# ScalarE takes Q's high part ahead of two casts in the steps of an attention head loop

## The chip, the cores and the metric

The kernel runs on one core of a Trainium2 chip. The metric is the device time of one execution in microseconds (us); for several executions the median stands.

## What is computed

Four layers run one after the other, each with a layer norm ahead of it and a residual behind it, on x of 2 x 512 x 256: an attention with 3 heads of width 256, a feed-forward layer with ternary weights, a causal attention with 16 heads of width 128, and a product in int8. The change lies in the third:

```
q = einsum('bpd,hde->bphe', x, W_Q) + b_Q        # k and v alike
scores = einsum('bqhe,bkhe->bhqk', q, k) / sqrt(128)
scores = where(causal, scores, -100000.0)
attn = softmax(scores, axis=-1)
z = einsum('bkhe,bhqk->bqhe', v, attn)
out = einsum('bqhe,hed->bqd', z, W_O) + b_O
```

## The kernel before

Every product of fp32 numbers is made of three passes over numbers that are split into a high and a low part (`split_mm`, L401 to L403): high with high, low with high, high with low. ScalarE writes the high part (a rounded copy), VectorE or GpSimd subtracts it from the source to get the low part. TensorE needs both.

The third layer runs in 32 steps, `window(w)`, w = 0 to 31: one head of one batch half in each. Inside a step no order is left to a scheduler: for TensorE, ScalarE and VectorE a list of marks (`PE_ORDER`, `ACT_ORDER`, `DVE_ORDER`) says what each does, one after the other; each engine has one queue and waits on semaphores in it. Steps 1 to 25 are the steady ones. The marks that count here, for step w:

- S0 to S3: the scores of step w+1, four blocks of 128 rows with 128 to 512 columns. TensorE multiplies (L689 to L696), VectorE masks them and takes the maximum (`max1`, L1483, tile SM), ScalarE takes the exponential (`exp1`, L963, tile PR).
- Q0, K1, V2: the projections for step w+2. TensorE multiplies (`project_qk`, `project_v`), ScalarE writes the high part (`project_hi`, Q_hi and K_parts on L957, V_hi on L954), VectorE the low part (`project_lo`, L1468, V_lo on L1465, which comes one step later as W2). Two PSUM banks take turns, so a projection waits until the low part of the one before the last is written: V2 waits for Q_lo of its own step, K1 for V_lo of the step before.
- C3, C2, C1, C0: the high parts of the turned probabilities of step w-1 (`moved_hi`, L974, PT_hi from MV). C3 waits for the transfer that brings MV. GpSimd writes the low parts in the same order (`moved_low`, L1154, PT_lo).
- B0: the attention product of step w-1 (`attend`), which waits for all four low parts; then ScalarE writes Z_hi (L980) and VectorE Z_lo (Z0 of the next step).
- U0 to U3: VectorE turns blocks of normalised probabilities into BT (`turn_blocks`, L1502). SP stores BT to DRAM and loads it back turned, as MV, one step later (L446, L452). GpSimd normalises ahead of that (`normalise`, L1138 to L1147).
- O0: the output projection of an earlier step. G0 to G3: in some steps VectorE splits weights of the next pair of heads (`load_a`, L1404 to L1408, `load_b`), GpSimd writes a part of their low halves (`split_a`, L1110) behind PT_lo and ahead of the normalisation. K's and V's projections wait for those.

TensorE's order in a steady step is S0 Q0 S1 S2 O0 K1 S3 V2 B0 (no O0 in steps 1 and 2), ScalarE's is S0 C3 C2 Q0 S1 C1 C0 S2 K1 S3 V2 B0, VectorE's begins S0 Z0 U2 U3 W2 S1 Q0 S2. A step starts here with S0 on TensorE. Step 7 starts at 249.47 us, step 8 at 258.72, step 9 at 268.61.

Of the kernel before, what the change touches and what calls it, by code (L numbers as in the profile page):

```python
# [63 lines left out]
def build(nc, x, wq0, wk0, wv0, fcT, fcb, wupT, wgateT, wdownT, pack1, bias_all, bo1, qw, qb, out):  # L64
    ctx = ExitStack()
    with ctx:
# [190 lines left out]
        def steps(text):  # L257
            return [(step[0], int(step[1])) for step in text.split()]
# [1 line left out]
        FIRST_MOVED, LAST_MOVED = 0, WINDOWS - 7  # L260
        STEADY_PE = (steps("S0 Q0 S1 S2 O0 K1 S3 V2 B0"),
                     steps("S0 Q0 S1 S2 O0 K1 S3 V2 B0"))
        STEADY_ACT = (steps("S0 C3 C2 Q0 S1 C1 C0 S2 K1 S3 V2 B0"),
                      steps("S0 C3 C2 Q0 S1 C1 C0 S2 K1 S3 V2 B0"))
        STEADY_DVE = (steps("S0 Z0 U2 U3 W2 S1 Q0 S2 O0 G0 G1 G2 G3 R0 S3 K1 U0 U1 R1"),
                      steps("S0 Z0 U2 U3 W2 S1 Q0 S2 O0 G0 G1 G3 R0 S3 K1 G2 U0 U1 R1"))
        EVEN_PE = steps("T0 T1 S0 O0 T2 T3 S1 Q0 S2 O1 K1 A0 S3 V2")
# [11 lines left out]
            WINDOWS - 2: steps("T0 T1 S0 S1 O0 S2 T2 T3 S3 O1"),  # L279
            WINDOWS - 1: steps("T0 T1 B0 T2 A0 T3 O0 A1 O1 I0 I1")}  # L280
        ACT_ORDER = {w: STEADY_ACT[w % 2] for w in range(1, LAST_MOVED + 1)} | {
            1: steps("S0 C3 C2 Q0 S1 C1 C0 S2 K1 S3 V2 B0"),
            0: steps("W2 S0 S1 Q0 S2 K1 S3 V2"),
            WINDOWS - 6: steps("T0 T1 S0 C3 C2 C1 C0 S1 T2 Q0 S2 T3 K1 B0 S3 A0"),
            WINDOWS - 5: EVEN_ACT,
# [1436 lines left out]
```

## Time and profile before

| | us |
|---|---|
| three runs: median (lowest, highest) | 506.07 (506.07, 508.27) |
| the profiled execution | 507.92 |
| its span, first to last instruction | 506.1 |
| TensorE, VectorE, ScalarE, GpSimd busy | 482.0, 379.1, 293.5, 281.9 |

The granted clock of TensorE is 0.994 of full speed on average. In a row of the order in time the columns are start, duration, engine, line and operation, output and input tiles, partitions x elements, count; in brackets stands the idle time before it and what ended it. In a row of waits: who waited for whom, us in total, how often, the longest.

### The profile page before, as it was taken

The numbers are of one execution on the slowest core, as the hardware profiler recorded it, in microseconds if no ns is written. First come the engines' busy times: TensorE is split into PE (matmuls) and PEld (weight loads), VectorE is DVE, ScalarE is ACT, GpSimd is POOL, SyncE is SP. The second block draws the span as 40 slices with busy tenths as digits, with TensorE's granted clock in tenths as the row PEclk, the third lists the DMA queues.
The fourth block names the chain that finished last, engine by engine and source line by source line (L and its number), as shares of the span: only waits on it lengthen the run. The fifth ranks groups of instructions, "written<-read, shape, count | busy, mean of one in ns | idle before, by whom it ended". The sixth has DMA issues, their size and how long they took to land.

```text
span 506.1 us, 8910 instructions
## 1 busy us (share of the span) xinstructions
PE 482.0 (95%) x3020; PEld 429.4 (85%) x3020; DVE 379.1 (75%) x967; ACT 293.5 (58%) x690; POOL 281.9 (56%) x378
## 2 busy tenths in 40 slices
PE   8999999999999978899999999999999989999973
PEld 7888998899888856789989989999889989899962
DVE  2676886775746577778878878888778896677887
ACT  2356336535454646586667667776766756655643
POOL 1344234422755456686677677786677796512243
PEclk9999999999999999999999999999999999999997
DMA  8900000000010017565665665655765645000002
GB/s 270 378 29 2 1 0 1 0 1 1 24 41 1 0 53 185 157 179 143 180 178 148 182 171 148 192 169 139 205 163 154 192 140 156 2 1 1 2 0 83
DMA packets 54380, 51.58 MB, mean 102 GB/s; under 512 B 3520, under 2 KB 49728, under 8 KB 54336
## 3 DMA queue, kind: packets, MB, share of 16 engines
q1 hardware_dynamic: 53248, 49.98, 34.4%
q10 hardware_dynamic: 1088, 1.05, 0.6%
q8 instruction: 24, 0.39, 0.3%
q14 instruction: 20, 0.16, 0.1%
HBM read 32.92 MB, written 18.09 MB: 101 GB/s over the span
## 4 chain that ended last, share of the span: by engine, by line
PE 68%; DVE 11%; DMA 7%; POOL 4%; issue 4%; ACT 4%; SPq 1%; DVEq 0%; POOLq 0%; ACTq 0%
PE bank L401 18%; PE bank L403 17%; PE bank L402 17%; DMA MV<-turned_dram 3%; PE bank L696 2%; PE bank L694 2%; PE bank L695 2%; POOL HID_lo L1123 2%; DMA turned_dram<-BT 2%; DMA Wv_sb<-wv 2%; DVE SM L1483 1%; PE bank L624 1%; PE bank L623 1%; ACT E L882 1%; DVE XN L1212 1%
## 5 line engine op out<-in xcount | busy, mean ns | idle before, releaser
L1154 POOL TENSOR_TENSOR PT_lo<-MV,PT_hi 128x512 fp32r<-128x512 f32 (+1 forms) x104 | 91.3, 910 | 51.9 <-ACT PT_hi L974 51.7
L963 ACT ACTIVATE PR<-SM,nmax 128x128 f32<-128x128 f32 (+3 forms) x128 | 72.0, 563 | 64.2 <-DVE nmax L1483 63.4
L1099 POOL TENSOR_TENSOR E_lo<-E,E_hi 128x512 fp32r<-128x512 f32 x24 | 31.0, 1295 | 53.7 <-ACT E_hi L887 46.6
L1483 DVE CUSTOM_DVE_ANT_0 SM<-bank,causal 128x384 f32<-128x384 f32 (+3 forms) x102 | 53.9, 529 | 8.8 <-PE bank L696 6.7
L401 PE MATMUL bank<-XT_hi,W_hi 128*128 128x512 f32 x128 | 52.3, 408 | 5.5 <-DVE V_lo L1465 4.1
L974 ACT CAST PT_hi<-MV 128x512 fp32r<-128x512 f32 (+1 forms) x104 | 42.1, 453 | 20.0 <-DMA MV<-turned_dram 19.8
L1502 DVE STREAM_TRANSPOSE BT<-PR 128x128 f32<-128x128 f32 (+1 forms) x104 | 48.1, 492 | 6.3 <-POOL PR L1138 4.6
L403 PE MATMUL bank<-XT_hi,W_lo 128*128 128x512 f32 x128 | 50.5, 394 | 0.0
L402 PE MATMUL bank<-XT_lo,W_hi 128*128 128x512 f32 x128 | 50.2, 392 | 0.0
L403 PE MATMUL bank<-PT_hi,V_lo 128*128 128x128 f32 (+3 forms) x130 | 41.5, 319 | 0.0
L402 PE MATMUL bank<-PT_lo,V_hi 128*128 128x128 f32 (+3 forms) x130 | 41.5, 319 | 0.0
L401 PE MATMUL bank<-PT_hi,V_hi 128*128 128x128 f32 (+3 forms) x130 | 40.5, 312 | 0.9 <-POOL PT_lo L1154 0.7
L882 ACT ACTIVATE E<-bank,nmax 128x512 f32<-128x512 f32 x24 | 16.5, 687 | 41.5 <-DVE nmax L1285 41.3
L401 PE MATMUL bank<-W_hi,XT_hi 128*128 128x256 f32 x128 | 36.3, 283 | 2.3 <-DVE Q_lo L1468 2.1
L401 PE MATMUL bank<-WO_hi,Z_hi 128*128 128x256 f32 x128 | 36.0, 282 | 2.0 <-DVE Z_lo L1517 2.0
L1468 DVE SCALAR_TENSOR_TENSOR Q_lo<-bank,bias,Q_hi 128x512 fp32r<-128x512 f32 x32 | 24.0, 749 | 17.3 <-ACT Q_hi L957 17.0
L402 PE MATMUL bank<-W_lo,XT_hi 128*128 128x256 f32 x128 | 35.7, 279 | 0.0
L403 PE MATMUL bank<-W_hi,XT_lo 128*128 128x256 f32 x128 | 35.7, 279 | 0.0
L403 PE MATMUL bank<-WO_hi,Z_lo 128*128 128x256 f32 x128 | 35.6, 278 | 0.0
L402 PE MATMUL bank<-WO_lo,Z_hi 128*128 128x256 f32 x128 | 35.6, 278 | 0.0
L694 PE MATMUL bank<-K_parts,Q_hi 128*128 128x384 f32 (+3 forms) x102 | 34.9, 342 | 0.0
L980 ACT ACTIVATE Z_hi<-bank,bias 128x512 fp32r<-128x512 f32 x31 | 21.4, 689 | 21.9 <-PE bank L403 21.9
(186 smaller groups left out, 1599.2 us busy)
## 6 DMA issues: line engine op xcount, KB each, us to landing
MV<-turned_dram SPq DMA_DIRECT2D x104, 160.0 KB, 3.2
turned_dram<-BT SPq DMA_DIRECT2D x26, 384.0 KB, 3.0
stage<-pack SPq DMA_DIRECT2D x32, 256.0 KB, 3.9
turned_dram<-BT SPq DMA_DIRECT2D x26, 256.0 KB, 3.3
X<-x SPq DMA_DIRECT2D x2, 512.0 KB, 8.9
wraw<-wupT SPq DMA_DIRECT2D x1, 1024.0 KB, 9.2
wraw<-wgateT SPq DMA_DIRECT2D x1, 1024.0 KB, 11.1
wraw<-wdownT SPq DMA_DIRECT2D x1, 1024.0 KB, 13.4
```

The lines of the kernel that those rows point to most:

```text
L401: pe.matmul(dst, a_hi, b_hi, start=first, stop=False, skip_group_check=share)
L402: pe.matmul(dst, a_hi, b_lo, start=False, stop=False, skip_group_check=share)
L403: return pe.matmul(dst, a_lo, b_hi, start=False, stop=last, skip_group_check=share)
L694: pe.matmul(dst[:, 0:n], Q_hi[:, slot, cols], K_hi[:, slot, 0:n], start=True, stop=False)
L882: act.activation(E0[:, m, :], bank[i % 3][:], ACT.Exp, bias=nmax0[:, m:m + 1], scale=1.0, accum_out=sum0[:, m:m + 1]).then_inc(s0_exp, 1)
L963: act.activation(PR[:, c, 0:(c + 1) * P], SM[:, c % 2, 0:(c + 1) * P], ACT.Exp, bias=nmax1[:, c:c + 1], scale=-1.0, accum_out=sum1[:, c:c ...
L974: act.copy(by_quad(PT_hi[w % 2], c), moved_part(w, c)).then_inc(mv_hi, 1)
L1099: pool.tensor_tensor(E0_lo[:, m, :], E0[:, m, :], E0_hi[:, m, :], ALU.subtract).then_inc(e0_lo, 1)
L1154: pool.tensor_tensor(by_quad(PT_lo[w % 2], c), moved_part(w, c), by_quad(PT_hi[w % 2], c), ALU.subtract).then_inc(mv_lo, 1)
L1468: ins = dve.scalar_tensor_tensor(lo[:, w % 2, :], src, bias1[:, p, 2 * which + h:2 * which + h + 1], hi[:, w % 2, :], ALU.add, ALU.subtract)
L1483: dve.tensor_tensor_reduce(SM[:, c % 2, 0:n], s_bank(w, c)[:, 0:n], mask, 1.0, HIGHEST, ALU.add, ALU.min, nmax1[:, c:c + 1]).then_inc(s_ma ...
L1502: dve.transpose(BT[w % 2][:, :, moved_blocks(c), :].rearrange("p j b c -> p b j c"), PR[:, c, 0:(c + 1) * P].rearrange("p (b j c) -> p b j ...
```

## The change

In the lists of ScalarE for steps 1 to 25, Q0 moves from behind C3 and C2 to the place ahead of them. The other engines' lists stay, and so do all instructions and semaphores. Step 0 and steps 26 to 31 have lists of their own, which stay.

```diff
-        STEADY_ACT = (steps("S0 C3 C2 Q0 S1 C1 C0 S2 K1 S3 V2 B0"),
-                      steps("S0 C3 C2 Q0 S1 C1 C0 S2 K1 S3 V2 B0"))
+        STEADY_ACT = (steps("S0 Q0 C3 C2 S1 C1 C0 S2 K1 S3 V2 B0"),
+                      steps("S0 Q0 C3 C2 S1 C1 C0 S2 K1 S3 V2 B0"))
...
         ACT_ORDER = {w: STEADY_ACT[w % 2] for w in range(1, LAST_MOVED + 1)} | {
-            1: steps("S0 C3 C2 Q0 S1 C1 C0 S2 K1 S3 V2 B0"),
+            1: steps("S0 Q0 C3 C2 S1 C1 C0 S2 K1 S3 V2 B0"),
```

## Rows read from the trace of the kernel before

**Rows 1.** Busy time by engine, from the page: us, share, instructions.

```profile
PE 482.0 (95%) x3020; PEld 429.4 (85%) x3020; DVE 379.1 (75%) x967; ACT 293.5 (58%) x690; POOL 281.9 (56%) x378
```

**Rows 2.** Waits of TensorE over the span.

```profile
PE bank L401 <- DVE V_lo L1465: 4.2, 5, 1.5
PE bank L401 <- DVE Q_lo L1468: 2.1, 4, 1.1
...
PE bank L401 <- POOL PT_lo L1154: 0.7, 2, 0.6
```

**Rows 3.** Waits of all engines over the span.

```profile
ACT PT_hi L974 <- DMA MV<-turned_dram: 19.8, 20, 2.2
...
DVE Q_lo L1468 <- ACT Q_hi L957: 17.0, 15, 2.4
```

**Rows 4.** Steps 8 and 7 as stretches: bounds, length, busy time of each engine.

```profile
258.72:268.61 9.89, 9.69 (x62) 8.47 (x61) 7.64 (x22) 6.36 (x16) 6.52 (x11) 1.00 0.84 221
249.47:258.72 9.25, 9.25 (x62) 8.47 (x61) 7.22 (x19) 6.37 (x16) 5.71 (x9) 1.00 0.60 170
```

**Rows 5.** Order in time: end of step 7 (first row), then step 8.

```profile
256.87 0.39 PE L401 MATMUL bank<-PT_hi,V_hi 128*128 128x512 f32 x1
...
262.51 1.03 ACT L974 CAST PT_hi<-MV 128x512 fp32r<-128x512 f32 x2 [2.15 <-DMA MV<-turned_dram]
...
263.21 3.38 POOL L1154 TENSOR_TENSOR PT_lo<-MV,PT_hi 128x512 fp32r<-128x512 f32 x4 [2.93 <-ACT PT_hi L974]
...
263.45 0.68 ACT L957 ACTIVATE Q_hi<-bank,bias 128x512 fp32r<-128x512 f32 x1
...
264.17 0.75 DVE L1468 SCALAR_TENSOR_TENSOR Q_lo<-bank,bias,Q_hi 128x512 fp32r<-128x512 f32 x1 [1.68 <-ACT Q_hi L957]
...
265.07 0.36 PE L401 MATMUL bank<-W_hi,XT_hi 128*128 128x256 f32 x1 [0.20 <-DVE Q_lo L1468]
...
266.64 0.51 PE L401 MATMUL bank<-PT_hi,V_hi 128*128 128x512 f32 x1
```

**Rows 6.** Order in time: step 9; the first row is the last matmul of Q0.

```profile
270.04 0.39 PE L403 MATMUL bank<-XT_hi,W_lo 128*128 128x512 f32 x1
...
270.15 1.02 ACT L974 CAST PT_hi<-MV 128x512 fp32r<-128x512 f32 x2
...
272.42 0.51 ACT L963 ACTIVATE PR<-SM,nmax 128x256 f32<-128x256 f32 x1 [0.66 <-DVE nmax L1483]
...
270.84 2.27 POOL L1154 TENSOR_TENSOR PT_lo<-MV,PT_hi 128x512 fp32r<-128x512 f32 x2 [1.52 <-ACT PT_hi L974]
273.39 1.38 POOL L1154 TENSOR_TENSOR PT_lo<-MV,PT_hi 128x256 fp32r<-128x256 f32 x2 [0.28 <-ACT PT_hi L974]
275.73 1.31 POOL L1110 TENSOR_TENSOR W_lo<-stage,W_hi 128x512 fp32r<-128x512 f32 x1 [0.97 <-DVE W_hi L1408]
...
276.04 0.39 PE L401 MATMUL bank<-PT_hi,V_hi 128*128 128x512 f32 x1
```

**Rows 7.** Order in time: step 5, its first two casts and GpSimd's weight split.

```profile
232.68 1.03 ACT L974 CAST PT_hi<-MV 128x512 fp32r<-128x512 f32 x2
...
238.11 1.31 POOL L1110 TENSOR_TENSOR W_lo<-stage,W_hi 128x512 fp32r<-128x512 f32 x1 [0.97 <-DVE W_hi L1408]
```

**Rows 8.** Order in time: steps 1 and 2; last, one piece of the chain.

```profile
196.05 4.01 POOL L1154 TENSOR_TENSOR PT_lo<-MV,PT_hi 128x512 fp32r<-128x512 f32 x4 [2.53 <-ACT PT_hi L974]
...
197.00 0.75 DVE L1468 SCALAR_TENSOR_TENSOR Q_lo<-bank,bias,Q_hi 128x512 fp32r<-128x512 f32 x1 [1.82 <-ACT Q_hi L957]
...
200.42 1.30 POOL L1110 TENSOR_TENSOR W_lo<-stage,W_hi 128x512 fp32r<-128x512 f32 x1 [0.36 <-DVE W_hi L1408]
...
206.24 0.47 PE L401 MATMUL bank<-XT_hi,W_hi 128*128 128x512 f32 x1 [1.46 <-DVE V_lo L1465]
...
210.12 5.31 DMA MV<-turned_dram
```

**Rows 9.** Order in time: step 24 on TensorE.

```profile
414.42 0.47 PE L401 MATMUL bank<-XT_hi,W_hi 128*128 128x512 f32 x1 [1.29 <-DVE V_lo L1465]
```

## Prediction

> **What bounds the kernel now.** I read the page's busy shares first, then the waits of TensorE, then the waits of all engines, then the busy time of single steps, and last the order in time on each engine inside four steps. TensorE is busy 95% of the span [rows 1], so a moved ScalarE instruction can only buy back idle time of TensorE. The waits of TensorE are short: 4.2 us for V's low part (5 times), 2.1 us for Q's low part (4 times), 0.7 us for the low part of the probabilities (2 times) [rows 2]. The other engines look much worse: VectorE waits 17.0 us for ScalarE's Q_hi, in 15 steps, and ScalarE's casts wait 19.8 us for the moved probabilities, in 20 of 26 steps [rows 3]. The first of these is what the change is aimed at: Q_hi stands in ScalarE's queue behind casts that wait for a transfer, although Q's product has long been there.
>
> A step that waits for nothing takes 9.25 us (step 7), step 8 took 9.89 us [rows 4]. TensorE reaches the attention product, the last of its step, 256.87 - 249.47 = 7.40 us after the start in step 7 [rows 4, 5]. Step 8 starts at 258.72. Its casts start at 262.51, 3.79 us in, after 2.15 us of waiting for the transfer; Q_hi follows at 263.45, Q_lo at 264.17 after 1.68 us of idle VectorE, and V's projection at 265.07, held 0.20 us by Q_lo [rows 5]. So far this reads like a stall that the change removes. But GpSimd works on PT_lo from 263.21 for 3.38 us, to 266.59, and the attention product starts at 266.64 [rows 5]. Of the two things that the attention product needs, PT_lo is the later. The casts lead to it with a fixed lag: 266.64 - 262.51 = 4.13 us. The limit follows: a cast that starts more than 7.40 - 4.13 = 3.27 us after its step's start delays TensorE, and a V projection 0.2 us earlier only waits longer at the next instruction.
>
> **What the change removes, adds and moves.** Nothing is added or removed. In steps 1 to 25 Q_hi goes ahead of two casts. The casts are busy 1.03 us, yet Q_hi starts 263.45 - 262.51 = 0.94 us after them, so neighbours overlap by 0.09 us, and Q_hi with its 0.68 us pushes what follows by 0.59 us [rows 5]. ScalarE issues no transfer there, so no queue of SP or GpSimd is passed. New is a wait: both casts now stand behind Q's projection on TensorE.
>
> *Steps with a late transfer* (1, 3, 8, 12, 18, 20: the casts wait longest there, 2.2 us at most [rows 3]). Q's projection ends about 1.83 us into a step (in step 9 its last matmul ends at 270.04 + 0.39 = 270.43, start 268.61 [rows 4, 6]). Q_hi then falls into the 2.15 us that ScalarE idled, and the casts start with the landing as before. V's projection no longer waits, PT_lo ends at the same time. Gain: 0. VectorE is freed up to 1.7 us earlier, which nobody on the path needs, with one exception below. It stays at zero while the casts lead to the attention product with the 4.13 us.
>
> *Steps with an early transfer.* Step 9 is the extreme: the casts ran without a wait at 270.15, 1.54 us in. Now Q_hi comes first. For the hand-over from TensorE I take the 0.05 us that lie between PT_lo's end and the attention product in step 8 [rows 5]; the casts start at 270.43 + 0.05 + 0.59 = 271.07, 2.46 us in, 0.92 us later. That is 0.8 us under the limit of 3.27, so TensorE does not see it. What else is late? The exponentials of S1 start at 272.42 because they wait for VectorE, while the casts end at 272.1: not moved. GpSimd starts 0.92 us later, 270.84 + 0.92 = 271.76, its first two instructions end 2.27 us later at 274.03; the 0.28 us wait before the last two is swallowed, and it ends at 274.03 + 1.38 = 275.41. In this step GpSimd next splits a weight at 275.73, and it had waited 0.97 us for VectorE's W_hi before that [rows 6]. So even there 0.3 us of cover is left, and the attention product (276.04) has 0.6 us. Step 5 starts at 249.47 - 2 x 9.25 = 230.97; its casts move from 232.68 to 233.43, by 0.75 us, and GpSimd had waited 0.97 us as well [rows 7]: 0.2 us of cover, the smallest; 13, 17, 21 and 23 have more. Cost: 0, and if the cover were gone, the price is in the slower rival.
>
> *The exception, step 1.* Q_lo waits 1.82 us for Q_hi (197.00), and behind it on VectorE stand the weight splits of this step. GpSimd ends PT_lo at 196.05 + 4.01 = 200.06, but starts its weight split at 200.42, because W_hi comes late; from there it goes to the turned blocks, V_lo of step 2, and TensorE stands still 1.46 us before 206.24 [rows 8]. With Q_lo 1.8 us earlier W_hi is there in time, and the split starts with the end of PT_lo: 0.36 - 0.02 = 0.34 us earlier. The same chain leads on into the store and the transfer that step 3 waits for (5.31 us in the chain [rows 8]), so the 0.34 us are kept through step 3. The bounds are 0, if PT_lo ends later by as much, and 1.46 us, the whole stall. I take 0.34, since PT_lo's end at 200.06 stands directly behind.
>
> *Step 24.* A like stall of 1.29 us stands here before K's projection [rows 9]. Its transfer was early, and in step 23, where the chain begins, I find no wait of Q_lo. Bounds 0 and 0.1 us; I take 0.
>
> Sum: 0.34 us, in round figures 0.4 with the few hundredths of step 24. The profiled execution took 507.92 us (span 506.1, 1.8 us around it) and would take 507.5. It is 1.85 us above the median of the three runs, 506.07; the same subtraction gives 505.7.
>
> The port between VectorE and GpSimd is the one size that I can't read off. In step 1 PT_lo took 4.01 us and in step 8, with no weight split on VectorE, 3.38 us [rows 5, 8]: a difference of 0.63 us. The Trainium skill (SBUF — State Buffer, Who interferes with whom) says that "A DVE instruction with two SBUF inputs contends with a GpSimd instruction that reads SBUF"; the two durations agree with it, and as the splits move 1.8 us earlier, by that rule they still fall inside PT_lo and only meet other instructions of it.
>
> **The rivals.**
>
> *Q_lo is what bounds (0.08).* For it: the page names Q_lo as the releaser of TensorE. Of the 2.1 us the longest (1.1 us) lies in step 0, whose order is not changed [rows 2]. 1.0 us are left, and with the 0.4: 504.7 us. Against it speaks PT_lo's end in step 8.
>
> *Transfers fall otherwise (0.11).* A landing decides six steps. In the chain it took 5.31 us at step 3 [rows 8]. If the shifted start lets them land early, each gives back 0.5 us (7.92 against 7.40 in step 8), 3 us in all: 503.1 us (0.07). If as many land later by the same, 508.7 us (0.04). No row speaks for either, the stores hang on TensorE's own pace.
>
> *The port (0.10).* Splits and PT_lo of step 1 cost each other 0.63 us more or less: 505.1 to 506.3 us. Moving the splits does not take them out of PT_lo's time, so the middle is kept.
>
> *Nothing is moved that matters (0.05).* 506.1 us.
>
> *Slower: the casts come too late (0.06).* Place: behind Q_hi in the steps with early transfers. Point of decision: casts more than 3.27 us into the step delay the attention product; in the weight steps 5, 9, 13, 17, 21 already 0.2 to 0.3 us beyond my time make GpSimd late for the turned blocks, and then V_lo late for K's projection. With the hand-over 1 us longer than taken, GpSimd is 0.7 us late. I estimate that half of it reaches TensorE in five steps and all of it in step 24, where V_lo is already late: 5 x 0.35 + 0.7 = 2.5 us, plus 0.2 us in some of the others: 508.9 us with the gain of step 1 gone. For it: the smallest cover is a few tenths. Against it: Q_hi's start is fixed by TensorE, which is steady.
>
> **How the numbers follow.** The forecast itself has 0.60, at 505.7 us, with 505.3 to 506.1 from its own bounds. The three runs of before lie 2.2 us apart, which belongs into the range as well. It reaches down past 504.7, not to 503.1, and up past the port's 506.3, not to 508.7: 504.2 to 507.6 us. A difference under 0.5% (2.5 us) cannot be told from no change for this kernel. Only the early landings are faster by more, 0.07; slower by more are the slower rival and the late landings, 0.09; within is 0.84.
>
> **What would show it.** Right: Q_hi starts about 1.9 us into every step from 1 to 25; the wait of VectorE for Q_hi falls from 17.0 us to 5 or 6, what lies before and behind the changed steps; TensorE's wait for Q_lo falls to the 1.1 us of step 0, and a wait for PT_lo (4.13 us behind the casts) stands in its place in steps 8, 12, 18 and 20; the casts never start before 2.4 us in; GpSimd's split in step 1 starts directly behind PT_lo, and the stall in step 2 is 1.1 us. Wrong: PT_lo ends after 7.3 us in a step whose transfer was early; the stall in step 24 over 1.3 us; the casts of step 8 starting elsewhere than 3.8 us in.

## The result

The change makes the kernel slower by 0.22%: the median of 20 runs is 507.48 us against 507.01 us for 20 runs of the kernel before, the ratio 1.0022 (95% interval 1.0012 to 1.0033). By that ratio the loss is about 1.1 us, in place of the 0.3 to 0.4 us gained that were forecast; it is not the ratio of the two medians, which lie only 0.47 us apart (the means lie 0.93 us apart). The profiled execution of the changed kernel took 506.95 us with a span of 505.2 us, 1.0 us less than the profiled one of before. Single executions of either kernel lie 2.5 to 3 us apart, so the time of one says nothing here; what can be read in one are the steps.

TensorE is as busy as before, and its waits have changed places. These are the lines that answer to [rows 1] to [rows 3]; the columns are the same.

```profile
PE 481.3 (95%) x3020; PEld 430.0 (85%) x3020; DVE 384.2 (76%) x967; ACT 293.9 (58%) x690; POOL 281.8 (56%) x378
```

```profile
PE bank L401 <- DVE V_lo L1465: 4.3, 7, 1.4
...
PE bank L401 <- POOL PT_lo L1154: 1.2, 2, 0.7
PE bank L401 <- DVE Q_lo L1468: 1.1, 1, 1.1
```

```profile
DVE Q_lo L1468 <- ACT Q_hi L957: 5.5, 5, 2.4
...
ACT PT_hi L974 <- DMA MV<-turned_dram: 4.8, 7, 1.4
```

The waits that the change aims at are nearly gone. TensorE waits for Q_lo once, in step 0 (2.1 us and 4 times before), and VectorE waits 5.5 us for Q_hi in place of 17.0. But TensorE waits 7 times for V_lo in place of 5, and VectorE is busy 384.2 us in place of 379.1, although it has the same 967 instructions. That is where to look: two of its lines take 4.8 of the 5.1 us. For L1404, the first split of weights, the view of one line gives the lowest, the median and the longest duration in ns; first the kernel before, then the changed one.

```profile
L1404 DVE TENSOR_SCALAR W_hi<-stage x8: 409/420/562, 133.5 to 405.4; 128x512 fp32r<-128x512 f32 x8
```

```profile
L1404 DVE TENSOR_SCALAR W_hi<-stage x8: 414/970/989, 133.4 to 404.2; 128x512 fp32r<-128x512 f32 x8
```

The same instruction takes 0.96 to 0.99 us in steps 5, 9, 13, 17, 21 and 23, in place of 0.42 (0.53 and 0.56 in steps 21 and 23). The other line is the cast of W_O's weights, L1417: 0.99, 0.87, 0.99 and 0.97 us in steps 3, 7, 15 and 19, where it took 0.51 to 0.57. Again before, then changed:

```profile
L1417 DVE CAST WO_hi<-stage x8: 412/530/575, 187.0 to 433.1; 128x512 fp32r<-128x512 f32 x8
```

```profile
L1417 DVE CAST WO_hi<-stage x8: 414/710/987, 186.9 to 432.3; 128x512 fp32r<-128x512 f32 x8
```

This one costs TensorE nothing that shows: steps 4 and 8, behind two of the slow casts, took 9.25 and 9.29 us; steps 16 and 20 were longer, with late transfers. The loss comes with L1404. Step 9 of the changed kernel, in order of time by engine (it starts at 266.42; [rows 6] answer to it):

```profile
268.28 0.69 ACT L957 ACTIVATE Q_hi<-bank,bias 128x512 fp32r<-128x512 f32 x1 [0.23 <-PE bank L403]
268.87 1.02 ACT L974 CAST PT_hi<-MV 128x512 fp32r<-128x512 f32 x2
270.23 0.51 ACT L963 ACTIVATE PR<-SM,nmax 128x256 f32<-128x256 f32 x1 [0.34 <-DVE nmax L1483]
...
269.56 3.57 POOL L1154 TENSOR_TENSOR PT_lo<-MV,PT_hi 128x512 fp32r<-128x512 f32 x4 [3.08 <-ACT PT_hi L974]
...
271.79 1.34 POOL L1154 TENSOR_TENSOR PT_lo<-MV,PT_hi 128x256 fp32r<-128x256 f32 x2
...
274.10 1.30 POOL L1110 TENSOR_TENSOR W_lo<-stage,W_hi 128x512 fp32r<-128x512 f32 x1 [0.97 <-DVE W_hi L1408]
...
271.85 0.96 DVE L1404 TENSOR_SCALAR W_hi<-stage 128x512 fp32r<-128x512 f32 x1
272.85 0.83 DVE L1406 SCALAR_TENSOR_TENSOR W_lo<-stage,W_hi 128x512 fp32r<-128x512 f32 x1
273.60 0.41 DVE L1408 CAST W_hi<-stage 128x512 fp32r<-128x512 f32 x1
...
279.11 0.65 DVE L1465 TENSOR_TENSOR V_lo<-bank,V_hi 128x512 fp32r<-128x512 f32 x1
```

The casts start 2.45 us in, GpSimd's third piece of PT_lo at 271.79, and VectorE's weight split at 271.85, 0.06 us behind it; the split takes 0.54 us more. Before, VectorE reached the same place, 5.42 us into the step, with GpSimd's third piece nearly through (it began at 273.39, 4.78 us in [rows 6]). GpSimd does not even see its own lateness: it still waits 0.97 us for W_hi, as before, only that W_hi comes 0.54 us later. From there everything is late: GpSimd's normalisation, the turned blocks, and V_lo of step 10, which ends at 279.76. K's projection starts there at 279.91, 4.21 us in; in the kernel before it starts 3.97 us into that step. First the changed kernel, then the one before:

```profile
279.91 0.47 PE L401 MATMUL bank<-XT_hi,W_hi 128*128 128x512 f32 x1
```

```profile
281.86 0.40 PE L401 MATMUL bank<-XT_hi,W_hi 128*128 128x512 f32 x1
```

The stretches show it too: steps 8 and 10 of the changed kernel, then step 10 of the kernel before.

```profile
257.13:266.42 9.29, 9.29 (x62) 8.50 (x61) 7.53 (x22) 6.60 (x16) 7.23 (x13) 1.00 0.68 193
...
275.70:285.29 9.59, 9.52 (x62) 8.56 (x61) 7.82 (x23) 6.55 (x17) 9.11 (x15) 1.00 0.57 162
```

```profile
277.89:287.18 9.29, 9.29 (x62) 8.50 (x61) 7.56 (x23) 6.48 (x16) 8.56 (x14) 1.00 0.66 175
```

Steps 6, 10, 14, 18 and 22, each behind a step with weight splits, took 9.68, 9.59, 9.62, 9.63 and 9.64 us from start to start, where a step that waits for nothing takes 9.25 to 9.29: 1.8 us in all. In steps 14 and 18 the casts were late as well (3.52 and 3.55 us in), so a part of their loss would be there without the collision. The stall of step 24 went from 1.29 [rows 9] to 1.37 us.

```profile
413.63 0.47 PE L401 MATMUL bank<-XT_hi,W_hi 128*128 128x512 f32 x1 [1.37 <-DVE V_lo L1465]
```

Step 1, the one with the forecast gain, answers to [rows 8]:

```profile
195.01 4.19 POOL L1154 TENSOR_TENSOR PT_lo<-MV,PT_hi 128x512 fp32r<-128x512 f32 x4 [1.61 <-ACT PT_hi L974]
199.17 1.29 POOL L1110 TENSOR_TENSOR W_lo<-stage,W_hi 128x512 fp32r<-128x512 f32 x1
...
204.96 0.47 PE L401 MATMUL bank<-XT_hi,W_hi 128*128 128x512 f32 x1 [1.03 <-DVE V_lo L1465]
```

GpSimd's split follows PT_lo at once, and the stall of step 2 shrank from 1.46 to 1.03 us. But PT_lo takes 0.18 us longer there, 4.19 us in place of 4.01.

### The profile page after: what moved, and what is told of

It reads as the page before. It is cut to its first block, busy times and chain, and to the rows that moved or that the text cites. A ratio compares the mean times of both kernels' runs of the same rounds, so it can differ in the third digit from the quotient of the medians.

```text
span 505.2 us, 8910 instructions
## 1 busy us (share of the span) xinstructions
PE 481.3 (95%) x3020; PEld 430.0 (85%) x3020; DVE 384.2 (76%) x967; ACT 293.9 (58%) x690; POOL 281.8 (56%) x378
## 4 chain that ended last, share of the span: by engine, by line
PE 61%; DVE 16%; POOL 7%; DMA 5%; issue 5%; ACT 4%; SPq 1%; DVEq 0%; POOLq 0%; ACTq 0%
PE bank L401 17%; PE bank L402 16%; PE bank L403 16%; POOL HID_lo L1123 2%; POOL PT_lo L1154 2%; PE bank L696 2%; PE bank L694 2%; PE bank L695 2%; DMA turned_dram<-BT 2%; DVE SM L1483 2%; DVE BT L1502 2%; DMA Wv_sb<-wv 2%; DMA MV<-turned_dram 2%; DVE V_lo L1465 1%; ACT PR L963 1%
## 5 line engine op out<-in xcount | busy, mean ns | idle before, releaser
L694 PE MATMUL bank<-K_parts,Q_hi 128*128 128x384 f32 (+3 forms) x102 | 34.9, 342 | 0.0
L695 PE MATMUL bank<-K_parts,Q_hi 128*128 128x384 f32 (+3 forms) x102 | 34.0, 334 | 0.0
```

Of the source, the lines that this page charges most:

```text
L694: pe.matmul(dst[:, 0:n], Q_hi[:, slot, cols], K_hi[:, slot, 0:n], start=True, stop=False)
L695: pe.matmul(dst[:, 0:n], Q_hi[:, slot, cols], K_lo[:, slot, 0:n], start=False, stop=False)
```

## The experiments

Theory A (port): GpSimd's third piece of PT_lo, later because the casts are later, blocks VectorE's first weight split; VectorE's lateness makes V_lo late one step on. Against it: B, the new order costs a little in every step; C, transfers land later; D, it is Q_hi and Q_lo being early that hurts; and the plainest one, GpSimd's own lateness, without VectorE. All ratios are to the kernel before, which ran in turn with them on the same chip. In the edited kernels the line numbers of the same instructions are a few higher.

### One part of the change: all steps but the weight steps

```diff
+        ACT_ORDER |= {w: steps("S0 C3 C2 Q0 S1 C1 C0 S2 K1 S3 V2 B0") for w in (5, 9, 13, 17, 21, 23)}
```

> Q0 goes ahead of C3 and C2 in all steps of 1 to 25 but 5, 9, 13, 17, 21 and 23, in which VectorE splits weights. Theory A (port): in the changed kernel GpSimd is still busy with the third piece of PT_lo when VectorE starts the first weight split (L1404), which then takes 0.97 us in place of 0.42; V_lo of the next step is late by as much, and TensorE loses 0.3 to 0.4 us in steps 6, 10, 14, 18 and 22, 1.9 us in all with step 24. Here L1404 stays at 0.42 us in these steps, steps 6, 10, 14, 18 and 22 take 9.25 to 9.3 us unless a transfer is late, and the time is that of the changed kernel less 1.9 us: 0.5 to 1 us under the kernel before, ratio about 0.998. Rival B (order): the casts behind Q0 cost a little in every step; then this has some 19/25 of the loss of the changed kernel, ratio about 1.0015. Rival C (transfers): the loss is in landings that fall later; ratio about 1.002, with more steps in which the attention product waits for PT_lo.

Measured: ratio 0.9985 (0.9965 to 1.0004), 506.73 us. The median of that line is 418 ns. Steps 6, 10, 18 and 22 took 9.29, 9.28, 9.28 and 9.31 us, step 14 took 9.78 with a late transfer. The loss is gone with six of 25 steps; that speaks against B and C, whose 1.0015 and 1.002 lie outside the interval. L1417 still takes 0.97 to 0.99 us in steps 3, 11, 15 and 19 of this kernel, so it is not what cost the time.

### The other part: the weight steps alone

```diff
+        ACT_ORDER |= {w: steps("S0 Q0 C3 C2 S1 C1 C0 S2 K1 S3 V2 B0") for w in (5, 9, 13, 17, 21, 23)}
```

> The counterpart: Q0 goes ahead of the casts in steps 5, 9, 13, 17, 21 and 23 alone. Theory A (port): L1404 takes 0.97 us in these six, the steps behind them are 0.3 to 0.4 us longer, and the time is 1.9 us over the kernel before, ratio about 1.0035 to 1.004, more than the changed kernel has. Rival B (order): 6/25 of the loss of the changed kernel, ratio about 1.0005. Rival C (transfers): no more than 1.001.

Measured: ratio 1.0016 (0.9995 to 1.0037), 508.32 us against 506.93. The steps show theory A, all five with early transfers:

```profile
L1405 DVE TENSOR_SCALAR W_hi<-stage x8: 410/966/990, 133.9 to 405.6; 128x512 fp32r<-128x512 f32 x8
```

```profile
239.89:249.50 9.61, 9.54 (x61) 8.59 (x61) 7.82 (x23) 6.57 (x17) 9.12 (x15) 1.00 0.54 149
277.50:287.15 9.65, 9.46 (x61) 8.51 (x61) 7.87 (x24) 6.74 (x17) 9.14 (x15) 1.00 0.59 162
315.01:324.60 9.59, 9.52 (x62) 8.56 (x61) 7.82 (x23) 6.68 (x17) 9.11 (x15) 1.00 0.61 163
352.79:362.38 9.59, 9.51 (x61) 8.55 (x61) 7.83 (x23) 6.57 (x17) 9.11 (x15) 1.00 0.57 158
390.50:400.16 9.66, 9.46 (x62) 8.51 (x61) 7.88 (x24) 6.63 (x17) 9.18 (x15) 1.00 0.59 160
```

These are steps 6, 10, 14, 18 and 22: 1.7 us above 9.28 together. The ratio is below the forecast of 1.0035, with that inside its interval; by itself it settles nothing.

### The casts late, Q_hi late as well

```diff
+        ACT_ORDER |= {w: steps("S0 E0 C3 C2 Q0 S1 C1 C0 S2 K1 S3 V2 B0") for w in (5, 9, 13, 17, 21, 23)}
...
+                    elif kind == "E":
+                        act.wait_ge(pj_psum, 3 * (w + 2) + 1)
+                        act.activation(XN[:, 0:2, :].rearrange("p t d -> p (t d)"), causal[:], ACT.Identity,
+                                       bias=bias1[:, 0, 0:1], scale=1.0)
```

> The order of the kernel before, but in steps 5, 9, 13, 17, 21 and 23 ScalarE does one more instruction ahead of C3 and C2: it waits for Q0's product as Q_hi does and has its shape (128x512, Identity with a bias), but reads a constant and writes a tile that nobody reads. Q_hi stays behind the casts. So the casts are as late as in the changed kernel, about 2.47 us into the step, and Q_hi is not early. Theory A (port): what counts is that the casts, and with them PT_lo, are later: L1404 takes 0.97 us as in the changed kernel, steps 6, 10, 14, 18, 22 are longer by 0.3 to 0.4 us (or more, as Q_lo is late too), ratio 1.0035 or more. Rival D: the loss comes from Q_hi and Q_lo being early (VectorE then does other work beside GpSimd): L1404 stays at 0.42 us and the ratio at 1.000.

Measured: ratio 1.0028 (1.0008 to 1.0047), and steps 6, 10, 14, 18 and 22 took 9.77, 9.68, 9.62, 9.81 and 9.72 us. But L1404 (here L1409) took 0.55 us, not 0.97: a miss. Step 5 of this kernel starts at 229.26:

```profile
233.39 0.75 DVE L1473 SCALAR_TENSOR_TENSOR Q_lo<-bank,bias,Q_hi 128x512 fp32r<-128x512 f32 x1 [0.36 <-ACT Q_hi L958]
...
235.13 0.55 DVE L1409 TENSOR_SCALAR W_hi<-stage 128x512 fp32r<-128x512 f32 x1
```

Q_lo waited, VectorE came to the split 5.87 us in, 0.44 us later than in the other kernels, and GpSimd's piece was nearly through. 0.44 us of start and 0.13 us of duration make 0.57 us, as much as the collision costs. So this run does not tell A from a plain lateness of VectorE. It shows the second half of the chain: some 0.55 us lost on VectorE by the end of the first split, from whatever cause, costs TensorE 0.34 to 0.44 us one step on (steps 10, 14 and 22; in steps 6 and 18 the casts came 3.65 and 3.71 us in as well). Nor does it decide on rival D: Q_lo is late here, which is a cause of its own.

### Less work for GpSimd in the changed kernel

This kernel leaves out most of the last two pieces of PT_lo in the weight steps; it keeps low parts of an earlier step there.

```diff
-                    pool.tensor_tensor(by_quad(PT_lo[w % 2], c), moved_part(w, c), by_quad(PT_hi[w % 2], c),
-                                       ALU.subtract).then_inc(mv_lo, 1)
+                    n = 1 if c < 2 and w + 1 in (5, 9, 13, 17, 21, 23) else QUAD
+                    pool.tensor_tensor(by_quad(PT_lo[w % 2], c)[:, :, :, 0:n], moved_part(w, c)[:, :, :, 0:n],
+                                       by_quad(PT_hi[w % 2], c)[:, :, :, 0:n], ALU.subtract).then_inc(mv_lo, 1)
```

> The changed kernel, in which GpSimd leaves out most of the two last pieces of PT_lo (blocks of 256 and 128 columns: one column of 32 is kept in each) in steps 5, 9, 13, 17, 21 and 23, so that these low parts are those of an earlier step. The casts are as late as in the changed kernel, but GpSimd is done with PT_lo about 1 us earlier. Theory A (port): VectorE's first weight split starts at 5.43 us into the step and finds GpSimd idle, takes 0.42 to 0.5 us, and the stalls of steps 6, 10, 14, 18 and 22 go: 1.9 us less than the changed kernel, ratio to the kernel before about 0.998. Rival B or D (the order on ScalarE itself, or Q being early): the late V_lo stays, ratio about 1.002.

Measured: ratio 0.9976 (0.9959 to 0.9994), 505.77 us. Step 9 starts at 267.89; the split is 5.43 us in, as in the changed kernel, and takes 0.45 us:

```profile
271.04 2.79 POOL L1155 TENSOR_TENSOR PT_lo<-MV,PT_hi 128x512 fp32r<-128x512 f32 x4 [3.08 <-ACT PT_hi L974]
```

```profile
273.32 0.45 DVE L1405 TENSOR_SCALAR W_hi<-stage 128x512 fp32r<-128x512 f32 x1
```

Steps 6, 10, 14, 18 and 22 took 9.24 to 9.29 us. ScalarE's order and the times of its casts are those of the changed kernel, and Q_hi is as early as there (Q_lo starts 3.69 us into step 9 in this kernel, in the changed one and in the one before), so what cost the time is GpSimd's work beside the split. Rivals B and D fall here.

### More work for GpSimd in the kernel before

```diff
+                    if c == 2 and w + 1 in (5, 9, 13, 17, 21, 23):
+                        pool.tensor_tensor(XN[:, 2, 0:240].rearrange("p (b i q) -> p b i q", b=3, i=CT), moved_part(w, c)[:, :, :, 0:20],
+                                           by_quad(PT_hi[w % 2], c)[:, :, :, 0:20], ALU.subtract)
```

> The kernel before, with ScalarE's order untouched: only GpSimd does one subtraction more between the first and the second piece of PT_lo in steps 5, 9, 13, 17, 21 and 23 (240 columns, into a tile that nobody reads, some 0.7 us). So GpSimd's third piece begins ahead of VectorE's first weight split (5.43 us into the step), as in the changed kernel, but the casts and Q_hi keep their times. GpSimd itself has 0.97 us of waiting ahead of its own weight split, so its lateness alone is covered. Theory A (port): L1404 takes 0.85 to 1.0 us in place of 0.42, steps 6, 10, 14, 18 and 22 take 9.6 us in place of 9.25, ratio to the kernel before 1.003 to 1.004. Rival D or B (the loss comes with ScalarE's order): L1404 stays at 0.42, the steps at 9.25 and the ratio at 1.000.

Measured: L1404 took 0.94, 1.00, 0.73, 0.72 and 1.02 us in steps 5, 9, 13, 17 and 21, and steps 6, 10, 14, 18 and 22 took 9.60, 9.66, 9.40, 9.39 and 9.64 us: the longer the split, the longer the step behind it. In step 23 the split took 0.52 us (0.56 before), but the two behind it 1.11 and 0.68. Step 9, with GpSimd's third piece of PT_lo in the last row:

```profile
271.20 0.70 POOL L1155 TENSOR_TENSOR XN<-MV,PT_hi 128x240 f32<-128x240 f32 x1
271.86 2.32 POOL L1157 TENSOR_TENSOR PT_lo<-MV,PT_hi 128x384 fp32r<-128x384 f32 x3
...
272.83 0.75 POOL L1157 TENSOR_TENSOR PT_lo<-MV,PT_hi 128x256 fp32r<-128x256 f32 x1
```

```profile
272.86 1.00 DVE L1407 TENSOR_SCALAR W_hi<-stage 128x512 fp32r<-128x512 f32 x1
```

ScalarE's order is the old one and Q_lo has its old times, and the collision and its price are back. GpSimd's own lateness is covered: PT_lo ends 6.75 us into step 9, and GpSimd still waits until 7.71 for VectorE's W_hi. That settles the last rival. The ratio is 1.0014 (0.9996 to 1.0032), where the five steps, 1.3 us over 9.28, would make 1.0026; that lies inside. Its expectation of 0.85 to 1.0 us was missed in steps 13 and 17, where the casts were earliest and VectorE came later into GpSimd's piece.

Six traces (the kernel before, the changed one twice, and the second, third and fifth experiment) give this as a series. When the split started 0.00 to 0.07 us behind the start of GpSimd's third piece it took 0.96 to 1.02 us; 0.09 behind, 0.94; 0.30 to 0.32 behind, 0.72 or 0.73; 0.46 to 0.49 behind, 0.53 to 0.57; 0.64 or 0.65 behind, 0.42. Each time it ended 1.01 to 1.07 us behind the start of that piece, which itself is recorded with 0.73 to 0.76 us. The end of the split is set by the piece and not by its own start, as of an instruction that stands still until the piece is done.

### Cover for the chain: the second split on ScalarE

ScalarE idles 1.5 us behind K_hi in step 9, and 2.05 us in the changed kernel. Two kernels let it do the cast of L1408 for K's weights there, one with the new order, one with the old.

```diff
+        for w in (1, 5, 9, 13, 17, 21, 23):
+            at = ACT_ORDER[w].index(("K", 1)) + 1
+            ACT_ORDER[w] = ACT_ORDER[w][:at] + [("G", 1)] + ACT_ORDER[w][at:]
...
+                        act.wait_ge(ld_pack[1], 16 * q + 16)
+                        act.copy(W_hi[q % 2][:, 1, :, :].rearrange("p k e -> p (k e)"),
+                                 stage[:, W_COLS:2 * W_COLS]).then_inc(wa_act, 1)
```

VectorE leaves this cast out, and GpSimd waits for ScalarE's signal (`wa_act`) in its place.

> The changed kernel, and the high part of K's weights in steps 1, 5, 9, 13, 17, 21 and 23 is cast by ScalarE behind K_hi (it idles 2 us there) and not by VectorE (L1408, second of the three splits). L1404 is still hit by GpSimd. Theory A: it still takes 0.97 us, but VectorE has 0.4 us less to do behind it and GpSimd's weight split starts 0.8 us earlier, so that V_lo of the next step is in time: steps 6, 10, 14, 18 and 22 take 9.25 to 9.3 us, the stall of step 24 shrinks from 1.4 to about 0.8 us, that of step 2 by 0.3. Ratio to the kernel before 0.995 to 0.998. Rival B (the order costs by itself, away from the weight splits): those steps stay at 9.6 us, ratio 1.001 or more.

> The same move of the cast to ScalarE, with ScalarE's old order (C3, C2 ahead of Q0). Theory A: steps 6, 10, 14, 18 and 22 had no stall and gain nothing; the stalls of steps 24 and 2 shrink by 0.3 to 0.6 us each: ratio to the kernel before 0.998. If with this cover the new order is at least as fast as the old one, then it was the cover, not the order, that the change lost on: e6 is then 0.5 to 1 us under e7, what the order gives in step 1 and in the steps with late transfers.

Measured: new order 0.9978 (0.9957 to 0.9999), old order 0.9959 (0.9938 to 0.9981). With the new order the split still takes 0.97 us, steps 10, 14 and 22 took 9.28 or 9.29 us, and step 24 stalls 0.35 us for V_lo, but a new wait of 0.65 us for K_lo stands at its start. Steps 6 and 18 took 10.14 and 9.45; in step 6 TensorE waited 0.62 us for PT_lo behind a late transfer, and in step 18 the casts came 3.35 us in, past the 3.27 of the prediction, and the attention product 4.15 us behind them. Where the wait for K_lo comes from was not found out. With the old order GpSimd's weight split starts earlier, as it was meant to:

```profile
274.90 1.30 POOL L1122 TENSOR_TENSOR W_lo<-stage,W_hi 128x512 fp32r<-128x512 f32 x1 [0.67 <-ACT W_hi L1045]
```

So the lost time can be covered, but with the cover the new order was not found faster than the old one, where 0.5 to 1 us had been expected; the two intervals overlap.

### Does the new order give anything where it does no harm?

The first edit (all steps but the weight steps) with the cover, beside the old order with the cover and the changed kernel, on one chip.

> Two edits together: Q0 ahead of the casts in all steps of 1 to 25 but 5, 9, 13, 17, 21 and 23 (as in the first experiment), and the high part of K's weights cast by ScalarE behind K_hi in steps 1, 5, 9, 13, 17, 21 and 23. No collision at L1404 (0.42 to 0.56 us), no stall in steps 6 to 22, the stall of step 24 at 0.8 us. If the new order is worth anything by itself where it does no harm, this is 0.3 to 1 us faster than the same with the old order, ratio to the kernel before 0.994 to 0.996; if it is worth nothing there (the casts lead to the attention product, whatever Q does), it equals it, ratio 0.996.

> The old order with K's weights cast on ScalarE once more, beside the others on one chip: ratio to the kernel before 0.996, as before, 0.994 to 0.998.

> The changed kernel once more, on the same chip as the two before it: ratio 1.002, L1404 at 0.97 us in steps 5, 9, 13, 17, 21 and 23, steps 6, 10, 14, 18 and 22 at 9.6 us in this execution too, since the collision comes from fixed times inside a step and not from transfers.

Measured: 0.9977 (0.9958 to 0.9995) with the new order in the calm steps, 0.9964 (0.9944 to 0.9984) with the old one, 1.0022 (1.0001 to 1.0043) for the changed kernel; medians 505.72, 505.13 and 508.22 us. The new order gives nothing that can be measured in the steps other than these six. In this execution of the changed kernel the median of L1404 is 965 ns again, and steps 6, 10, 14, 18 and 22 took 9.54, 9.61, 9.60, 9.65 and 9.60 us: the collision does not hang on transfers. Step 5 is telling. The casts came 0.14 us later there than in step 9, the split started 0.11 us ahead of GpSimd's third piece, and it took 0.43 us. But the two behind it took 1.11 and 0.69 us in place of 0.83 and 0.41:

```profile
235.11 0.43 DVE L1404 TENSOR_SCALAR W_hi<-stage 128x512 fp32r<-128x512 f32 x1
235.58 1.11 DVE L1406 SCALAR_TENSOR_TENSOR W_lo<-stage,W_hi 128x512 fp32r<-128x512 f32 x1
236.61 0.69 DVE L1408 CAST W_hi<-stage 128x512 fp32r<-128x512 f32 x1
```

```profile
235.22 0.92 POOL L1154 TENSOR_TENSOR PT_lo<-MV,PT_hi 128x256 fp32r<-128x256 f32 x1
```

VectorE lost 0.57 us all the same, and step 6 was long. The old order with K's weights on ScalarE has the lowest ratio of all kernels, 0.4% under the kernel before in both measurements (1.8 to 2.1 us), and is faster than both kernels of the case.

## Why the prediction was wrong

The range held the median, the direction was wrong: no change with 0.4 us of gain was forecast, and the kernel lost 1.1 us. That the range held it is no merit of the sum. The forecast of 505.7 us was built on the median of three runs, 506.07, and twenty runs gave 507.01 for the same kernel; it was the width of the range that covered this and the loss. Its chances also add up by a slip: inside are 0.83, slower by more 0.10, where it says 0.84 and 0.09.

**What bounds the kernel** was read rightly. TensorE's wait for Q_lo in the steps with late transfers was covered by PT_lo: VectorE's wait for Q_hi fell to 5.5 us, TensorE's for Q_lo to the one of step 0, and nothing came of it. Two steps show it side by side, both with the casts 3.93 us in: step 12 of the fifth experiment, in the old order, where TensorE waits 0.26 us for Q_lo, took 10.02 us, and step 16 of the changed kernel, without that wait, 10.04. The attention product stands 4.14 us behind the casts in the latter, as the lag of 4.13 would have it. The kernels with and without the new order in the calm steps show the same.

**Steps with an early transfer: this is the step that failed.** Every time in it was right within 0.1 us (casts at 2.45 us in, PT_lo's end at 6.71 against 6.80), and so was GpSimd's wait of 0.97 us. (The cover of 0.2 us in step 5 was too small a figure: PT_lo ended at 6.73 there, 0.4 us ahead of the old start of the weight split.) What I asked was who waits for GpSimd. I did not ask what runs beside it.
**The slower rival** (0.06) had the place (weight steps, turned blocks, V_lo, K's projection) and nearly the price, 5 x 0.35 us where the trace has 1.8 us in five steps. Its condition was wrong: it was to begin with a cast later than I had worked out. It began at the very times of the forecast.

**Step 1** gave what was forecast, less a part: the split follows PT_lo, and the stall of step 2 is 1.03 us (1.1 forecast, 1.46 before). But the splits now meet larger pieces of PT_lo, and the attention product of step 1, which waits for PT_lo in both kernels, stands 4.93 us behind the casts in place of 4.76: 0.2 of the 0.4 us are given back. **Step 24** is 0.08 us worse, not 0 to 0.1 better: the collision of step 23 is in its chain.

**The rest of the sum.** 1.8 us lost in five steps and 0.1 in step 24 less 0.2 gained in steps 1 and 2 make 1.7 us; measured are 1.1 us (0.6 to 1.7). What fills the difference was not separated from the scatter of the transfers.

**The signs that I named** worked. "The stall in step 24 over 1.3 us" was one for a wrong forecast, and it came (1.37 us in both executions of the changed kernel), though 1.29 us before the change left it little room. So did "the casts of step 8 starting elsewhere than 3.8 us in": 2.68 in the profiled execution, but 3.75 in the second one, so that one told only of a landing.

## What to carry to other kernels

When an instruction is moved, its consumers get new times as well, also where they have cover: look for what they now run beside. VectorE and GpSimd are the pair to check, for GpSimd's work before or behind a VectorE copy, cast or scaling from SBUF. A wait that a view names as a stall is worth nothing as long as another operand of the next instruction comes later. And where the cover is thin, giving a piece of VectorE's chain to an engine that idles there was worth more (0.4%) than either order of ScalarE's queue.

## What the runs showed of the hardware

How far GpSimd's piece has come when VectorE's split starts decides over 0.55 us: nothing is lost at 0.64 us into a piece of 0.74, and 0.54 us at 0.06. Which of the two starts first changes who waits, and not VectorE's bill: 0.57 us with its split ahead by 0.11. That holds for the third piece; the fourth, smaller one begins 0.05 us behind the split in step 9 of the kernel before, and no split is slower for it. In step 1 both engines pay, VectorE's three splits with 0.47, 1.39 and 0.95 us (0.42, 0.83 and 0.41 in step 9 of the kernel before; 0.46, 1.11 and 0.67 in its step 1), GpSimd's PT_lo with 4.19 us in place of 3.38 without splits beside it:

```profile
196.12 0.47 DVE L1404 TENSOR_SCALAR W_hi<-stage 128x512 fp32r<-128x512 f32 x1
196.63 1.39 DVE L1406 SCALAR_TENSOR_TENSOR W_lo<-stage,W_hi 128x512 fp32r<-128x512 f32 x1
197.94 0.95 DVE L1408 CAST W_hi<-stage 128x512 fp32r<-128x512 f32 x1
```

And the steps with late transfers are not the same from one execution to the next: in the kernel before steps 1, 3, 8, 12, 18 and 20 were long, in the profiled execution of the changed kernel steps 16 and 20 (with late casts in 14 and 18 too), in its second one steps 3, 7, 8, 12 and 16. What sets a landing was not tried.
